# Feed-forward rows turned into columns by VectorE in 32x32 blocks instead of by TensorE

## The reference

```python
def attn(x):                                  # x is layer-normed
    q, k, v = split(x @ qkv_w.T)              # 16 heads of 16
    qw = exp(sum((q - centers)**2) * inv_var) # 16 splats a head
    kw = exp(sum((k - centers)**2) * inv_var)
    logits = einsum('bihs,bjhs,hs->bijh', qw, kw, amplitudes)
    return softmax(logits / temp, axis=2) @ v @ out_w.T

def ffn(x):                                   # x is layer-normed
    x_prev = shift(x, 1)                      # the token before, zeros first
    xr = mu_r * x + (1 - mu_r) * x_prev
    xk = mu_k * x + (1 - mu_k) * x_prev
    return sigmoid(xr @ W_r.T) * (relu(xk @ W_k.T)**2 @ W_v.T)

x = x + attn(layernorm(x))
x = x + ffn(layernorm(x))
```

## Time and profile before

| | |
|---|---|
| time, median of 3 runs | 2163.5 us (2162.55 to 2164.25) |
| the profiled execution's own time | 2162.0 us |
| its span | 2160.2 us |
| TensorE matmul busy | 2129.8 us, 99% |
| ScalarE busy | 2013.2 us, 93% |
| VectorE busy | 742.1 us, 34% |
| GpSimd busy | 386.5 us, 18% |
| granted TensorE clock | 0.998 |

### The profile page before, as it was taken

How to read it: one execution, slowest core, us unless ns; L and a number is a source line. 1 busy time by engine, 2 the same in 40 slices (tenths; PEclk the granted TensorE clock), 3 DMA queues, 4 the chain that set the end, 5 groups by cost and what they waited for, 6 DMA issues and landing times.

```text
span 2160.2 us, 52461 instructions
## 1 busy us (share of the span) xinstructions
PE 2129.8 (99%) x22996; PEld 975.8 (45%) x22996; DVE 742.1 (34%) x1684; ACT 2013.2 (93%) x2190; POOL 386.5 (18%) x486
## 2 busy tenths in 40 slices
PE   7999999999999999999999999999999999999999
PEld 5444444444444444444444444444444444444445
DVE  5324433233432432433323334324323223323225
ACT  3899999999999999999999999999999999999995
POOL 0244243333100142022101203320310000000000
PEclk9999999999999999999999999999999999999999
DMA  6554445353221334316131332523252141311111
GB/s 179 141 147 121 123 125 147 107 154 112 67 68 51 94 109 109 97 41 174 27 91 28 112 94 72 138 60 99 61 144 53 41 90 41 61 30 48 33 41 44
DMA packets 176232, 193.06 MB, mean 89 GB/s; under 512 B 88529, under 2 KB 108369, under 8 KB 175985
## 3 DMA queue, kind: packets, MB, share of 16 engines
q1 hardware_dynamic: 166720, 174.69, 29.3%
q0 software_dynamic: 7168, 14.69, 2.7%
q10 hardware_dynamic: 2096, 0.14, 0.1%
HBM read 98.90 MB, written 75.81 MB: 81 GB/s over the span
## 4 chain that ended last, share of the span: by engine, by line
PE 90%; ACT 7%; DVE 2%; issue 1%; DMA 0%; DVEq 0%
PE ps_pv L889 40%; PE ps_scores L870 27%; PE ps_step L917 17%; ACT probs L1214 6%; PE ps_step L938 2%; PE ps_scores L902 1%; PE ps_step L896 1%; PE ps_scores L907 1%; ACT weight L1278 0%; PE ps_scores L912 0%; PE ps_scores L911 0%; DMA x_prep<-x 0%; DVE weight L1478 0%; DVE ffn_stats L1381 0%; DVE h_ffn L1395 0%
## 5 line engine op out<-in xcount | busy, mean ns | idle before, releaser
L1214 ACT ACTIVATE probs<-ps_scores 128x1024 f32<-128x1024 f32 x2048 | 1941.1, 1030 | 82.7 <-PE ps_scores L870 56.4
L889 PE MATMUL ps_pv<-probs,vals 128*32 128x512 f32 (+5 forms) x10104 | 1079.8, 520 | 0.0
L870 PE MATMUL ps_scores<-q_aug,k_aug 49*128 49x512 f32 x4096 | 706.2, 442 | 8.1 <-ACT probs L1214 5.9
L870 PEld LDWEIGHTS ps_scores<-q_aug,k_aug 49*128 49x128 f32 x4096 | 331.2, 184 | 617.2 <-ACT probs L1214 563.6
L889 PEld LDWEIGHTS ps_pv<-probs,vals 128*32 128x32 f32 x10104 | 349.4, 139 | 201.1 <-issue 118.2
L1336 POOL DMA_DIRECT2D packed<-qk x224 | 113.5, 512 | 871.9 <-DVE qk L1501 850.2
L1341 POOL TENSOR_TENSOR packed<-qk 32x512 f32<-32x512 f32 x224 | 238.2, 1064 | 16.9
L1346 POOL TENSOR_TENSOR k_act<-k_act 128x512 f32<-128x512 f32 x28 | 29.5, 1054 | 817.8 <-DVE k_act L1504 817.8
L1567 DVE COPY o_raw<-ps_pv 128x512 f32<-128x512 f32 x63 | 43.6, 691 | 247.3 <-PE ps_pv L889 246.6
L1501 DVE COPY qk<-ps_step 128x512 f32<-128x512 f32 x56 | 38.7, 690 | 223.9 <-PE ps_step L917 223.9
L1478 DVE TENSOR_SCALAR weight<-ps_step,cen_sq 128x512 f32<-128x512 f32 x57 | 42.8, 750 | 198.0 <-PE ps_step L938 197.1
(11 more groups left out here) (207 smaller groups left out, 1126.6 us busy)
## 6 DMA issues: line engine op xcount, KB each, us to landing
k_aug<-k_parts SPq DMA_DIRECT2D x128, 192.0 KB, 5.0
q_aug<-q_parts SPq DMA_DIRECT2D x128, 192.0 KB
k_parts<-parts SPq DMA_DIRECT2D x32, 512.0 KB, 3.3
q_parts<-parts SPq DMA_DIRECT2D x32, 512.0 KB, 4.7
packed<-qk POOLq DMA_DIRECT2D x224, 64.0 KB, 2.2
x_ffn<-x SPq DMA_DIRECT2D x18, 512.0 KB, 4.8
k_parts<-parts SPq DMA_DIRECT2D x32, 256.0 KB, 4.0
q_parts<-parts SPq DMA_DIRECT2D x32, 256.0 KB, 5.3
```

The costliest lines, as they stand in the source:

```text
L870: mm = pe.matmul(ps_scores[:, g % RING, e, :], k_aug[rows, s % 2, pair, kt * P:(kt + 1) * P], q_aug[rows, u % 2, pair, :], start=True, sto ...
L889: mm = pe.matmul(ps_pv[32 * c:32 * c + 32, at], vals[:, s % 2, kt, :, c], probs[:, tick % PROB_SLOTS, c, at], start=(kt == 0), stop=(kt == ...
L1214: act.activation(probs[:, tick % PROB_SLOTS, 2 * pair:2 * pair + 2, :], ps_scores[:, g % RING, :, :], ACT.Exp).then_inc(probs_ready, 1)
```

## The change

The steps turn0 and turn1 leave TensorE's side work. In their place VectorE transposes `h_ffn` straight to `h2_t`, in 32x32 blocks. `turned(task, a)` takes the 32 token partitions starting at 32a, and in four instructions puts the dims 32b to 32b+31 of both halves and all four row groups (256 elements a partition) to the partitions from 32b. That is 16 instructions for a chunk, in the ticks end(out1) + 4, 5, 6 and 7, behind the leave and ahead of the mix in a tick's order. The mixes move from turn1's end to the ticks end(out1) + 8, 8, 9, 10, and r0 is ready 10 ticks behind out1's end. All else of VectorE's list keeps its ticks relative to the steps. The loop's planner lays the remaining steps with unchanged budgets.

```diff
+TURNED_TICKS = (4, 5, 6, 7)
+MIX_TICKS = 8
-FFN_STEPS = ("out0", "out1", "turn0", "turn1", "r0", "r1", "k0", "k1", "v0", "v1")
-FFN_AFTER = {"out1": (("out0", 0),), "turn0": (("out1", 4),), "turn1": (("turn0", 0),), "r0": (("turn1", 4),), "r1": (("r0", 0),),
+FFN_STEPS = ("out0", "out1", "r0", "r1", "k0", "k1", "v0", "v1")
+FFN_AFTER = {"out1": (("out0", 0),), "r0": (("out1", MIX_TICKS + 1),), "r1": (("r0", 0),),
...
-MIX_AT = beside((later(end(task, "turn1") + (1, 1, 2, 3)[part]), (task, part)) for task in FFNS if task != LAST_BUT for part in range(4))
+TURNED_AT = beside((end(task, "out1") + TURNED_TICKS[a], (task, a)) for task in FFNS if task != LAST_BUT for a in range(TT))
+MIX_AT = beside((later(end(task, "out1") + MIX_TICKS + (0, 0, 1, 2)[part]), (task, part)) for task in FFNS if task != LAST_BUT for part in range(4))
...
-                if name == "turn0":
-                    pe.wait_ge(ffn_ln, LN_STEPS * (n + 1))
                 if name == "r0" and first == 0:
-                    pe.wait_ge(mix_steps, MIX * n + 5)
+                    pe.wait_ge(mix_steps, MIX * n + TURNED + 4)
...
-                elif name.startswith("turn"):
-                    if index == 0:
-                        v.wait_ge(mix_steps, MIX * n)
-                        carry(task).then_inc(mix_steps, 1)
-                        v.wait_ge(mix_steps, MIX * n + 1)
-                    v.tensor_copy(h2_t[:, index, 1:1 + CHUNK], bank).then_inc(step_free, 1)
...
+            def turned(task, a):
+                n = FFN_NO[task]
+                tokens = slice(32 * a, 32 * a + 32)
+                if a == 0:
+                    v.wait_ge(mix_steps, MIX * n)
+                    carry(task).then_inc(mix_steps, 1)
+                    v.wait_ge(mix_steps, MIX * n + 1)
+                    v.wait_ge(ffn_ln, LN_STEPS * (n + 1))
+                for b in range(4):
+                    dims = slice(32 * b, 32 * b + 32)
+                    to = h2_t[dims, :, 1:1 + CHUNK].rearrange("p h (n t) -> p n h t", t=P)[:, :, :, tokens]
+                    of = h_ffn[tokens, :, :].rearrange("p n (h d) -> p n h d", d=P)[:, :, :, dims]
+                    v.transpose(to, of).then_inc(mix_steps, 1)
...
             def mix(task, part):
-                n = Count(MIX * FFN_NO[task] + 1 + 2 * part)
+                n = Count(MIX * FFN_NO[task] + TURNED + 2 * part)
                 which, half = divmod(part, 2)
-                v.wait_ge(step_free, STEP_NO[task, "turn1"] + 1)
...
+                for task, a in TURNED_AT.get(tick, ()):
+                    turned(task, a)
                 for task, part in MIX_AT.get(tick, ()):
                     mix(task, part)
```

More of the change, by code:

```diff
@@ L66 @@
 CREDIT = 1.5
-TURN_LOAD = 1.5
 FINISH = (0, 0.5, 1, 2)
@@ L134, in pieces_of @@
 def pieces_of(name):
-    return 1 if name.startswith("turn") else 4 if name.startswith("dist") else 8
+    return 4 if name.startswith("dist") else 8
 def load_of(name):
-    return TURN_LOAD if name.startswith("turn") else 0.5
+    return 0.5
 def crosses_unit(gap):
@@ L210, in ffn_step @@
             name = left[other][0] if left[other] else None
-            if name in ("out0", "out1") or (name in ("turn0", "turn1") and done(task, "v0")):
+            if name in ("out0", "out1"):
                 if tick >= ffn_ready(n + 1, name):
@@ L227, in lay_side_work @@
             for due, ready, task, name in sorted(step for step in (prep_step(), ffn_step(tick)) if step):
-                if tick >= ready and (room >= 1 or not name.startswith("turn")):
+                if tick >= ready:
                     now = task, name, 0
@@ L231, in lay_side_work @@
                     break
-        if now and gap % 2 == 0 and not now[1].startswith("turn"):
+        if now and gap % 2 == 0:
             room = min(room, share_of(gap, pair, (pieces_of(now[1]) - now[2]) / 2))
@@ L403, in work_in @@
     for task, name, part in PIECES_AT.get(name_of(gap), ()):
-        if part % 2 and found and found[-1][:2] == (task, name) and not name.startswith("turn"):
+        if part % 2 and found and found[-1][:2] == (task, name):
             found[-1] = task, name, part - 1, part
@@ L614, in preln_block @@
         max_stored = sem("max_stored")
-        MIX = 9
+        TURNED = 1 + 4 * TT
+        MIX = TURNED + 8
         MAX_TILES = KT * (HEADS * NC + 1)
@@ L993, in ffn_piece @@
                 index = int(name[-1])
-                if name.startswith("turn"):
-                    mm = turn(h_ffn, index, ps_step[:, :])
-                elif name.startswith("out"):
+                if name.startswith("out"):
                     mm = rows_in_quarters(attn, wout, index, first, last, 0)
```

## The result

The changed kernel takes 2196.3 us (median of 4 runs, 2195.2 to 2197.7) against 2163.4 us (4 runs): 1.0155 times the kernel before, with an interval of 1.0143 to 1.0167. It is 33 us slower. I had forecast 2166 us, and the range ended at 2178. The prediction was wrong in size, and it was wrong in where the time goes.

A forecast was written before the change was run, and what follows sets the result against it. TensorE was taken to bound the gaps with side work and ScalarE the empty ones. A gain of 7 us against 9.6 us from TensorE standing made +2.6 us, forecast as 2166 us, range 2154 to 2178.

The forecast's parts named there:

- The gain: On TensorE, 28 turn steps leave, 42 units of side work at 0.17 us each: 7 us back, bounds nothing and 16.
- The price of a transpose: On VectorE, 0.455 us for each of 224 transposes, 7.3 us a chunk; bounds 0.37 and 0.70 us each.
- In the others prep steps come first: Of 14 chunks, those without r0 close behind out1 have prep steps first, and no standing of TensorE was counted there.
- The nine chunks with r0 close behind: Before r0, TensorE stands 2.9 us in the first chunk, 2.8 in two, 0.4 in six: 10.9 us in sum.
- One of my own signs of being wrong: The prediction is wrong if out1 of most chunks ends elsewhere in its unit than assumed; no size given.
- The exchange rate of 0.88: Each us that TensorE stands costs 0.88 us of time, 1.36 over 1.55 at one late eviction of gate_in.
- The clock has no part in the sum: TensorE's clock stays at full speed in every stretch read, so no time was counted for it.
- TensorE waiting at r0's first piece for the mix: Expected sign: TensorE waits there for VectorE's mix, part of 11 us of waits, mostly in chunks one, five and nine.
- At side steps for VectorE's evictions: Expected sign: TensorE waits at side steps for VectorE to empty the bank, the other part of the 11 us.
- near 56: Expected sign: ScalarE's wait for scores from TensorE stays near 56 us, 56.4 before the change.
- Rival two: VectorE falls behind at r0 as transposes meet the leave: 2172.5 us for about six chunks, 2178.5 for nine; chance 0.28.
- Rival one: VectorE hides all the added work and only the 7 us gain is left: 2156.5 us; chance 0.25.

The follow-up runs named there:

- no_transposes: The changed kernel with its plan kept and the 224 transposes left out, so the feed-forward result isn't computed: 2157.0 us.
- planned14: The changed kernel with each transpose and mix placed by a planner where VectorE has room, r0 ready 15 ticks behind out1: 2158.9 us.
- burst_long: The kernel before plus 224 transposes of constant data to a spare buffer, sixteen in a row ahead of v1's eviction in 14 places: 2254.5 us.
- burst_short: The kernel before plus 224 transposes of constant data to a spare buffer, in fours ahead of 56 evictions: 2202.0 us.
- behind_v1: The changed kernel with its transposes moved to out1's end + 9 to 12 and the mix to + 13: 2200.1 us.
- planned12: The changed kernel with transposes and mixes placed by a planner where VectorE has room, r0 ready 13 ticks behind out1: 2172.7 us.

## Why the prediction was wrong, step by step

- **The gain** was right: 7 us forecast, 5.7 measured with the transposes left out.
- **The price of a transpose** was right: 0.468 us from start to start for 0.455, and 820 us busy for 817. The upper bound of 0.70 and the lower one of 0.37 are out. The Trainium skill's section on two Vector instructions with no wait between them, in VectorE: DVE Perf Modes, which the prediction set beside rows 9, is borne out.
- **"In the others prep steps come first", five chunks at nothing**: this is the step that failed first. Being late at r0 isn't the only way to be late. All side steps share `ps_step`, and the copies of the chunk before and of prep steps stand behind the block in VectorE's list. These five chunks hold 15.1 of the 28.2 us that the standing grew by (against `no_transposes`). The eighth chunk lost 9.1 us at ScalarE in one wait, and the sixth 4.3. I should have laid out the new plan, in which v1's copy comes at tick 9 nearly everywhere: it is fixed when the program is built, and both diff and planner were there to read.
- **The nine chunks with r0 close behind** were near in sum, 12.9 us for 10.9, and wrong one by one, so that is partly luck. The first has 4.68 us, 0.91 of it without transposes too, for 2.9; the fifth 1.42 + 3.47 for 2.8; the ninth 0.75 for 2.8, as out1 ends in tick 0 of a unit there and no longer in tick 12, so that its transposes no longer meet the leave; the tenth 0.49 for 0.4; the eleventh 1.99 for 0.4. I walked three of them on the old plan, even after noting that removed turn steps pull the next eviction up, "so to about 1734". One of my own signs of being wrong came true: out1 ends at another place in its unit in 12 of 14 chunks.
- **The exchange rate of 0.88** came from one stand of 1.55 us. It was near for short stands (1.02) and too low for those that the change makes (1.39 on average), where it leaves out the clock. Together: 28.2 x 1.39 = 39.3 instead of 10.9 x 0.88 = 9.6.
- **"The clock has no part in the sum"** was false for the changed kernel. Even the old trace had a sign of it, outside the stretches that I read: TensorE stood 1.99 us for a copy of `qk` until 231.33, and the 4 us behind that have a granted clock of 0.57.
- **"TensorE waiting at r0's first piece for the mix"** had the place and not the cause: 12.4 us there, 0.4 of it for the mix. "At side steps for VectorE's evictions" was right. ScalarE's wait went to 97.8 and not "near 56".
- **Rival two** had the right side and the right engine, with the leave and r0 as its place. Its time for six chunks, 2172.5, and for all nine, 2178.5, both lay too low, for the five chunks and for the clock. The rule of the Trainium skill that it cited (VectorE: DVE Perf Modes, "Rules for kernel authors"), TensorE for a 128x128 transpose, gave the right sign for this placement. It doesn't hold as a rule on this kernel: `planned14` does the same transposes on VectorE and beats both, the kernel before by 0.2% (0.9981, interval 0.9972 to 0.9990).
- **Rival one**, VectorE hides everything, 2156.5, is what `planned14` comes near with 2158.9. It was right about VectorE's capacity, which never was the question.

## What to carry to other kernels

An engine that is idle two thirds of the time can still be the bound when it works through one list in order and empties a buffer that the busy engine needs: ask not how busy it is, but what stands ahead of each eviction in its list, on the new schedule. Place added work in small pieces by the load of each stretch, behind nothing that others wait for; on one and the same plan of TensorE, the same 98 us of transposes gave times from 2200.1 us in a block at fixed ticks to 2158.9 placed by load. And price a stall by what the clock does behind it: short ones cost about their own time here, long ones about 1.5 times it.

## What the runs showed of the hardware

I hadn't expected TensorE's clock to move at all. It fell to 1.2 GHz behind stands of 6.88 and 2.77 us (changed kernel), 6.90 (`burst_long`) and 3.19 (`burst_short`). In the 41 stands of `burst_short`, 1.1 us on average, it fell twice, behind the 3.19 and behind one of 2.00 at 231.7 us, which the kernel before has too. The one of 2.77 us is in the sixth chunk, in these windows:

```profile
1159.00:1165.00 6.00, 3.23 (x44) 1.59 (x43) 5.70 (x12) 5.48 (x6) 0.00 (x0) 1.00 0.11 25
1165.00:1168.00 3.00, 3.00 (x24) 0.82 (x24) 2.89 (x5) 0.00 (x0) 0.00 (x0) 0.65 0.00 0
1168.00:1174.00 6.00, 6.00 (x72) 3.09 (x68) 1.30 (x2) 4.78 (x6) 0.00 (x0) 0.89 0.59 218
```

ScalarE lost 4.30 us by it, 1.5 times the stand. The length of a stand doesn't decide alone. These are two stands and the windows behind them, first in the changed kernel, then in `burst_long`:

```profile
1786.57 1.43 PE L920 MATMUL ps_step<-wr,mixed_r 128*32 128x256 f32 x16 [1.99 <-DVE gate_in L1511]
...
1786.50:1790.50 4.00, 3.94 (x28) 1.64 (x30) 3.90 (x9) 0.55 (x2) 0.00 (x0) 0.58 0.00 0
```

```profile
1983.73 1.50 PE L919 MATMUL ps_step<-wr,mixed_r 128*32 128x256 f32 x24 [3.16 <-DVE gate_in L1514]
...
1983.70:1988.00 4.30, 3.86 (x42) 1.63 (x46) 4.15 (x6) 0.79 (x1) 0.00 (x0) 1.00 0.47 145
```

Behind 1.99 us the clock was at 0.58 of full speed, and behind 3.16 us it stayed at 1.00. Nor do length and place together: all nine kernels without turn steps have a stand of 2.44 to 2.47 us in the first chunk, for the copy of `ps_pv` (`o_raw`) between 556.7 and 558.4 us, in each case behind 20 us in which TensorE was busy throughout. In six profiled executions the clock fell behind it (in `planned14` the 4 us behind have 0.50), in three it stayed at 1.00 (`no_transposes`, `behind_v1`, `planned12`). What decides, these runs leave open.

The transposes of 32x256 take 0.437 us where those of 128x256 in `burst_short` take 0.445: a quarter of the partitions makes an instruction no cheaper. That is why moving a 128x128 transpose to VectorE costs so much there: 28 turn steps were 16 us of TensorE, and 224 small transposes are 98 us of VectorE.
